# Four cross-attention layers on one core: the wide layers' slots doubled, the narrow layers' weighing in one run

## The reference, cut to what is computed

```python
# L0 (narrow): layer norms, attention, then a feed-forward part with GELU
qn, kn = norm(x), norm(ctx)
Q, K, V = qn @ wq + bq, kn @ wk + bk, kn @ wv + bv        # 256 -> 16 heads of 16
attn = softmax(Q @ K.T / 4);  x = x + (attn @ V) @ wo + bo
x = x + gelu(norm(x) @ w1 + b1) @ w2 + b2
# L1 (wide): RMS norm of the queries only, no scale, no bias
Q, K, V = rms(x) @ wq, ctx @ wk, ctx @ wv                 # 256 -> 16 heads of 64
x = x + (softmax(Q @ K.T) @ V) @ wo
# L2 (wide): rotary positions on Q and K, a mask on the keys, a layer norm at the end
Q, K = rope(x @ Wq), rope(ctx @ Wk);  V = ctx @ Wv
x = norm(x + (softmax(mask(Q @ K.T / 8)) @ V) @ Wo)
# L3 (narrow): as the attention of L0
```

## Time and profile before

| what | us |
|---|---|
| median of 3 runs (2110.45 to 2115.55) | 2113.66 |
| the profiled execution | 2111.77 |
| its span, first to last instruction | 2109.8 |
| TensorE busy (94%) | 1983.6 |
| VectorE busy (67%) | 1414.2 |
| ScalarE busy (60%) | 1276.3 |
| GpSimd busy (27%) | 562.3 |

### The profile page before, as it was taken

The page is one execution under the profiler, slowest core; times in us unless marked ns, Lnnn a source line. Parts: engine busy times, 40 slices in busy tenths (PEclk is TensorE's granted clock), DMA queues, the critical chain, the costliest instruction groups (busy, mean ns, idle before and its releaser), DMA issues. The chain is left out here.

```text
span 2109.8 us, 50608 instructions
## 1 busy us (share of the span) xinstructions
PE 1983.6 (94%) x18664; PEld 1642.0 (78%) x18664; DVE 1414.2 (67%) x2898; ACT 1276.3 (60%) x3249; POOL 562.3 (27%) x676
## 2 busy tenths in 40 slices
PE   7999996978999999999999999999999998899997
PEld 6777775977888888888777787877878876777786
DVE  4777875544545545555577887888788874677775
ACT  3777775545555555555556665666566653677775
POOL 3323320000000000000035755766666651000000
PEclk8999998999999999999999999999999998899999
DMA  5434442021000000000001000000000001344442
GB/s 165 154 125 139 145 131 101 7 73 38 16 8 9 15 9 8 15 9 8 16 1 51 10 15 11 9 10 17 9 10 10 9 1 34 108 131 131 124 124 70
DMA packets 72858, 109.63 MB, mean 52 GB/s; under 512 B 7052, under 2 KB 62508, under 8 KB 72620
## 3 DMA queue, kind: packets, MB, share of 16 engines
q1 hardware_dynamic: 72332, 105.88, 16.5%
q10 hardware_dynamic: 288, 0.51, 0.1%
HBM read 69.18 MB, written 37.19 MB: 50 GB/s over the span
## 5 line engine op out<-in xcount | busy, mean ns | idle before, releaser
L1516 ACT ACTIVATE wide_P<-PS,MX 100x361 f32<-100x361 f32 x512 | 288.3, 563 | 407.3 <-DVE MX L1634 407.3
L1634 DVE TENSOR_REDUCE MX<-PS 100x2 f32<-100x722 f32 x256 | 231.7, 905 | 148.0 <-PE PS L1386 146.5
L615 ACT ACTIVATE L_P<-PS,MX 100x361 f32<-100x361 f32 x512 | 252.7, 565 | 122.0 <-DVE MX L745 122.0
L745 DVE TENSOR_REDUCE MX<-PS 100x2 f32<-100x722 f32 x256 | 219.6, 899 | 45.2 <-PE PS L501 44.9
L1815 POOL TENSOR_TENSOR wide_AC<-wide_T,wide_COSM 128x362 f32<-128x362 f32 x128 | 130.1, 1016 | 336.3 <-ACT wide_T L1465 334.1
L513 PE MATMUL PP<-CON,L_P 100*128 100x100 f32 x1536 | 184.1, 257 | 26.4 <-DVE L_PT L752 17.5
L513 PEld LDWEIGHTS PP<-CON,L_P 100*128 100x128 f32 x1536 | 151.2, 144 | 48.4 <-ACT L_P L615 33.7
L1395 PE MATMUL PP<-CON,wide_P 100*128 100x100 f32 x1536 | 176.5, 251 | 0.0
L1395 PEld LDWEIGHTS PP<-CON,wide_P 100*128 100x128 f32 x1536 | 161.1, 142 | 9.0 <-issue 2.3
L1409 PE MATMUL PS<-wide_PT,wide_V 128*64 128x100 f32 (+1 forms) x3072 | 161.9, 254 | 0.0
L1409 PEld LDWEIGHTS PS<-wide_PT,wide_V 128*64 128x64 f32 (+1 forms) x3072 | 136.8, 137 | 31.0 <-issue 23.3
(11 more groups left out here) (242 smaller groups left out, 5355.2 us busy)
## 6 DMA issues: line engine op xcount, KB each, us to landing
strips<-L_KS SPq DMA_DIRECT2D x256, 90.5 KB
L_KA<-strips SPq DMA_DIRECT2D x64, 362.0 KB, 3.1
C<-ctx_t SPq DMA_DIRECT2D x32, 361.0 KB, 3.1
kept<-L_CTH SPq DMA_DIRECT2D x16, 361.0 KB, 4.7
kept<-L_CTL SPq DMA_DIRECT2D x16, 361.0 KB, 5.5
L_CTH<-kept SPq DMA_DIRECT2D x16, 361.0 KB, 4.2
L_CTL<-kept SPq DMA_DIRECT2D x16, 361.0 KB, 5.0
C<-in_ctx SPq DMA_DIRECT2D x8, 256.0 KB, 3.4
```

The lines of the kernel that those rows point to most:

```text
L615: nc.scalar.activation(P[:, (4 * g + j) % 8, 0:SK], PSB[0:SQ, j, 0:SK], ACT.Exp, bias=MX[:, s % 2, 4 * q + j:4 * q + j + 1], scale=1.0).th ...
L745: nc.vector.tensor_reduce(MX[:, s % 2, 4 * q + 2 * i:4 * q + 2 * i + 2], PSB[0:SQ, 2 * i:2 * i + 2, 0:SK], AX.X, ALU.max, negate=True).the ...
L1516: nc.scalar.activation(P[:, (2 * g + i) % 4, 0:SK], PS_[i][0:SQ, 0:SK], ACT.Exp, bias=MX[:, s % 2, h:h + 1], scale=1.0, accum_out=DEN[:, s ...
L1634: nc.vector.tensor_reduce(MX[:, s % 2, 2 * p:2 * p + 2], PSB[0:SQ, 0:2, 0:SK], AX.X, ALU.max, negate=True).then_inc(Z["maxed"], 1)
```

## The change

Wide layers: the loops run over double slots (s, d), d = 0 to 3, with two pairs each. TensorE: scores of pair 2G, scores of pair 2G + 1, weighing of the two pairs of the double slot before, the jobs `first` (two K tiles), transposes of pair 2G, the jobs `mid` (R, V, O), transposes of pair 2G + 1, the jobs `late` (two Q tiles in odd batches, X). The scores have four banks, and the transposes go into the bank from which the exponentials were read; scores of a pair wait for the unloads of the pair two before it. The three banks of jobs and `PO` are the same number as before. `PT` has four slots instead of six. VectorE and ScalarE follow the new order; both parts of the context's split stand at the end of d = 1. In L2 VectorE now does both maxima, all joins of the double slot before, `invert`, and only then the shuffles; and R of the same half batch is the first job of `mid` in the same double slot as its `invert`.

Narrow layers: `P1` and `P` are one job of 96 matmuls in `a_` of slot 1, and the Q tile of slot 0 stands behind it in `b_` of slot 1.

```diff
@@ narrow_layer, jobs_at(s, q), q == 0
-                    if even and 2 <= s < B:
-                        b_.append(("Q", s, 3))
-                    if not even and s + 1 < B:
-                        b_.append(("Q", s + 1, 1))
@@ q == 1
                     if s == 0:
                         a_.append(("B", 0, 0))
                     else:
-                        a_.append(("P1", s - 1, 0))
-                        b_.append(("P", s - 1, 0))
+                        a_.append(("P", s - 1, 0))
+                    if even and 2 <= s < B:
+                        b_.append(("Q", s, 3))
+                    if not even and s + 1 < B:
+                        b_.append(("Q", s + 1, 1))
@@@@@@ wide_layers
-            BANKS = [*PJ, PSB[:, 3, :]]
-            PO = PSB[:, 2, :]
+            BANKS = [*PJ, PP[1]]
+            PO = PP[0]
-            PT = local("PT", [128, 6, KV_TILES * SQ])
+            PT = local("PT", [128, 4, KV_TILES * SQ])
+            def jobs_at(s, d):
+                first, mid, late = [], [], []
+                if s + 1 < NS:
+                    first += [("K", s + 1, 2 * d), ("K", s + 1, 2 * d + 1)]
+                    if s % 2:
+                        late += [("Q", s + 1, 2 * d), ("Q", s + 1, 2 * d + 1)]
+                if s % 2 == 0 and d == 3 and s + 2 < NS:
+                    late.append(("X", s + 2, 0))
+                if d == 0 and s > 0:
+                    mid.append(("R", s - 1, 1))
+                if d == 0 and 0 < s < NS:
+                    mid.append(("V", s, 2))
+                if d == 1 and s > 0:
+                    mid.append(("O", s - 1, 0))
+                if d == 2 and s < NS:
+                    mid.append(("R", s, 0))
+                if d < 3 and s < NS:
+                    mid.append(("V", s, 3 + d))
+                if d >= 2 and s + 1 < NS:
+                    mid.append(("V", s + 1, d - 2))
+            def score_bank(g, i):
+                return PSB[:, 2 * (g % 2) + i, :]
@@ TensorE
-                            pe.wait_ge(Z["exped"], 2 * g)
+                            pe.wait_ge(Z["unloaded_even"], g - 1)
+                            pe.wait_ge(Z["unloaded_odd"], g - 1)
+                            scores(s, 2 * d)
+                            scores(s, 2 * d + 1)
+                        if 1 <= G <= 4 * NS:
+                            weigh(2 * G - 2)
+                            weigh(2 * G - 1)
+                        for key in first:
+                            job(key)
+                        if s < NS:
+                            turn(2 * G)
+                        for key in mid:
+                            job(key)
+                        if s < NS:
+                            turn(2 * G + 1)
+                        for key in late:
+                            job(key)
@@ VectorE
+                            maximum(2 * G)
+                            maximum(2 * G + 1)
+                        for key in turns_of(G - 1):
+                            join(key)
+                        if d == 0 and s:
+                            invert(s - 1, 1)
+                        if d == 2 and s < NS:
+                            invert(s, 0)
...
+                        for key in first:
+                            job(key)
+                        if s < NS:
+                            unload(2 * G)
+                        for key in turns_of(G - 1):
+                            rotated_low(key)
+                        for key in mid:
+                            job(key)
+                        if s < NS:
+                            unload(2 * G + 1)
...
+                        if d == 1 and s + 2 < NS:
+                            for k in range(KE):
+                                context_low(s + 2, k)
@@ ScalarE
+                            for n in range(4):
+                                exponential(2 * G + n // 2, n % 2)
+                        for key in first:
+                            job(key)
+                        for key in turns_of(G - 1):
+                            rotated_high(key)
+                        if s < NS:
+                            unload(2 * G)
```

More of the change, by code:

```diff
@@ L252, in narrow_layer @@
             PARTS = (0, 2, 1)
-            order = FIRST + [k for sl in SLOTS for part in jobs_at(*sl) for k in part if k[0] != "P1"]
+            order = FIRST + [k for sl in SLOTS for part in jobs_at(*sl) for k in part]
             job_no = {k: n for n, k in enumerate(order)}
@@ L440, in weigh @@
                         pe.wait_ge(Z["ones"], 1)
[L441 to L444, removed]
+                        pe.wait_ge(Z["unloaded_even"], NSLOT * s + 4)
+                        pe.wait_ge(Z["unloaded_odd"], NSLOT * s + 4)
+                        dst = begin(key)
+                        for q in range(NSLOT):
                             for t, r in enumerate(KV_ROWS):
@@ L449, in weigh @@
                                                             pt(NSLOT * s + q)[0:r, at:at + SQ], start=t == 0, stop=t == KV_TILES - 1)
-                        if half:
-                            last.then_inc(Z["made"], 1)
+                        last.then_inc(Z["made"], 1)
                     def normal_turn(key):
@@ L647, in _ @@
                         for key in a_:
[L648 removed]
+                            if key[0] not in "MP":
                                 job(key)
@@ L1732, in _ @@
                             scale(s - 1, 1)
-                        if p == 6 and s < NS:
+                        if d == 2 and s < NS:
                             scale(s, 0)
-                        for key in turns_of(g - 1):
-                            join(key)
-                        if p == 0 and s:
-                            invert(s - 1, 1)
-                        if p == 4 and s < NS:
-                            invert(s, 0)
-                        if not shuffles_first:
-                            for key in after_scores:
-                                job(key)
@@ L1762, in _ @@
-                        if p in (2, 3) and s + 2 < NS:
-                            context_low(s + 2, p - 2)
-                        for c in CHUNKS_AT.get((s, p), ()):
+                        if d == 1 and s + 2 < NS:
+                            for k in range(KE):
+                                context_low(s + 2, k)
+                        for c in CHUNKS_AT.get((s, d), ()):
                             split_low(c)
```

165 lines of the change are left out of this document (61 added, 104 removed).

## The result

The changed kernel has a median of 2152.07 us (2151.02 to 2159.25, 4 runs), against 2114.11 (2110.45 to 2115.55, 4 runs) beside it: ratio 1.0189, with an interval of 1.0164 to 1.0215. It is slower by 1.9%. Its profiled span is 2149.7 us, 39.9 more than before.

A forecast was written before the change was run, and what follows sets the result against it. TensorE was taken to bound L1 and L2, with VectorE close behind in L2. L1 -12, L2 about 0 and narrow layers +3 gave -9 us, from a median of 2113.7 to 2105 us; range 2065 to 2133.

The forecast's parts named there:

- The switches: Wide layers: one way into the scores and one out saved, 0.37 us per double slot, 47 us for 32 batches.
- the 0.25 that I had named as a sign of being wrong: Wide layers: the forecast is wrong if the gap between two pairs' scores is over 0.25 us.
- rival (4): Not described in the text given; one of the slower cases, sharing a chance of 0.36, and left out of the range.
- L1: Gain of 1.5 us less V's wait of 0.75 at d = 2 per batch; -12 us over 16 batches.
- L2, the gain: L2: a pair of batches gains 4.9 us, 3.0 from the switches and 1.9 from old idle time.
- L2, the waits: L2: new waits of R and V at d = 0 and 2, taken as 4.8 us per pair; net about 0.
- Rival (2): L2: joins held up beside GpSimd, 1.14 us instead of 0.55 for half of them; 24 us, 2129 us; chance 0.25.
- Rival (1): Waits hidden by VectorE's free time in L2; 2052 us, or 2080 with half of the waits; chance 0.15.
- Narrow layers, the step that failed: Narrow layers: one weighing run and the moved Q tile together cost +3 us, bounds -9 and +12.
- 96 matmuls already cover everything: Narrow layers, slot 1: the weighing run already covers the waits there, so the moved Q tile's 0.7 us come on top.

The follow-up runs named there:

- c5: c3, but with `RX` written early only in L2 and at its old place in L1; 2086.91 us, ratio 0.9872 to the kernel before.
- w4: w0 with the context's two parts split at d = 1 and d = 2, one each, instead of both at d = 1; 2125.14 us, ratio 1.0037.
- c3: w0 with `RX` written early, the context spread as in w4, and K's shuffles ahead of the Q joins; 2087.54 us, ratio 0.9863.
- n3: Kernel before with only the narrow layers' Q tile moved from slot 0 to slot 1, weighing still in two halves; 2128.84 us, ratio 1.0043.
- w2: w0 with `RX` written at the end of the double slot before, ahead of the joins; 2122.14 us, ratio 1.0032.
- w0: The changed kernel's wide layers alone, with the narrow layers of the kernel before; 2138.48 us, ratio 1.0090.

## Why the prediction was wrong, step by step

**The switches, mis-sized.** Right in kind: where scores follow other work than transposes, the second pair of scores follows at 0.17 without a gap, K after K as well. Wrong in size: I gave 0.37 us for a double slot. c5, where PE waits for 0.2 us in these 12 batches of L1, has 460.7 against 471.2: 0.22. The term was summed from gaps at four edges, as if what stands there afterwards had none. Its PE timeline in an even batch:

```profile
717.29 0.68 PE L1397 MATMUL PS<-CON,wide_P 100*128 100x100 f32 x6
717.90 0.41 PE L1390 MATMUL PS<-wide_KH,wide_QH 64*100 64x362 f32 x2
...
718.31 0.33 PE L1390 MATMUL PS<-wide_KH,wide_QL 64*100 64x362 f32 x2
718.58 0.41 PE L1390 MATMUL PS<-wide_KH,wide_QH 64*100 64x362 f32 x2
```

The scores now follow six transposes, and these take 0.61 us until the first score, while the same six take 0.46 ahead of V: the way in costs 0.15 here and cost 0.08 behind V. Behind transposes, in 18 of these 48 double slots, the second pair of heads also starts 0.27 after the first instead of 0.17. That is over the 0.25 that I had named as a sign of being wrong, and no run shows its cause. It is no full drain either, since L1 did get shorter, so rival (4) is out; that its 2152 us is the measured time is chance. What is missing, 0.37 - 0.22 = 0.15 for each of 128 double slots, is 19 of the 47 us that this term had promised.

**L1.** The wait of V for K's low part came, 14 times in L1 and up to 0.6 us, where 0.75 was taken, from the cause named: w4 removes it by spreading the context. Net 0.42 for a batch instead of 0.75. The total (-11.8 against -12) agrees by luck, since 5.4 us of it are the first batch.

**L2, the gain.** A pair of batches (L2 / 7.5) was to gain 4.9; by L1's price of a double slot it is 8 x 0.22 + 1.9 = 3.7. That price is carried over from L1. It fits PE's busy time in L2, 594.9 in c5 against 609.5 before, which is 0.24 for each of 60 double slots.

**L2, the waits.** Measured: 87.3 for a pair against 83.2, so waits of 4.1 + 3.7 = 7.8, where I took 4.8. R's and V's, all that I had, come to (21.4 + 11.6) / 7.5 = 4.4: right. Not foreseen were the scores behind VectorE's second unload, 13.6 / 7.5 = 1.8, and the clock behind a stall of 2 us, five falls of some 1.4 us, 0.9. The remaining 0.7 is in no wait that the profile names. I had followed VectorE's list to `RX` and not to its end, where the low parts and the unload stand.

**Rival (2)** had the right opponent at the wrong instruction. The joins were not held up: 525 and 390 ns for K and Q, against 555 and 617 before. The low parts were, 790 and 1066 ns against 610 and 649: over L2 the joins take 23 us less of VectorE's time than before and the low parts 40 more. My sum had no term for the low parts. **Rival (1)**, the waits are hidden, failed: R did wait, 15 times in L2. c3, with an L2 10 us under that of before, shows how much of it another order gives.

**Narrow layers, the step that failed.** "96 matmuls already cover everything" put them at the wrong side of the transposes. They stand ahead of the first transposes that use the bank, and the wait is behind these. Forecast +3, measured +21 in the two stages and 1.0092 alone. The other half of the working holds: in slot 0 nothing is gained without Q, and its 0.7 us come on top in slot 1, as n3 shows. By spans the forecast was 2100.8 and the measured 2149.7. Of these 48.9 us (47 in the medians) 18 are the narrow layers, 31 L2, 0 L1, -2 the last batch and 1 the way to the first wide score.

**What stays open.** How the unnamed 0.7 us of a pair are made up, and through which instruction an `RX` written earlier costs L1 0.26 us in a batch (w2 against w0): c5 shows only that it does. Why the second pair's scores come later behind transposes. Whether GpSimd costs L2 more by its lateness or by holding up the low parts: rotation products on an engine other than GpSimd would tell, and were not tried.

## What to carry to other kernels

Where two steps share a buffer, work between them is a cover for the engine that empties it; a job that is moved or merged takes its cover away, even when it costs nothing itself, so ask of each moved run not only how long it is but which two instructions it stood between. When VectorE's list is rearranged, follow it to the end of the slot, and look for every instruction that reads two SBUF tiles, the low parts here as well as the joins, what GpSimd does beside it in the new order, and what stands behind it. Edits of one in-order list don't add up: the early shuffles cost 13 us alone and gave 24 behind the early `RX`, so a second wait can be worked on only after the first has gone.

## What the runs showed of the hardware that I had not expected

- A longer ring made the kernel slower (657 to 665 us in L2): GpSimd's waiting protected part of VectorE's low parts of K, 0.79 us on average against 1.06.
- A way into 64-row matmuls cost 0.15 us behind transposes and 0.08 behind full matmuls, and behind transposes the second pair of them came 0.10 later as well.
- One stall of 2.03 us and another of 0.53, with 0.56 us of work between them, were followed by 3.3 us at a granted clock of 0.50. Batch 26 had a stall of 2.0 us too, and no fall.
